# Turning a later token tile's normalised rows, latents and rotary keys by three DMA transposes in place of nineteen on TensorE

## The reference

```python
xn = layernorm(x)
q  = rmsnorm(xn @ w_qa) @ w_qb          # 384 latents, 16 heads of 128 + 64
kv = xn @ w_kva                         # 128 latents and 64 rotary numbers
k_rope = kv[..., 128:] * cos + rotate_half(kv[..., 128:]) * sin
kv = rmsnorm(kv[..., :128]) @ w_kvb
scores = (q_nope . k_nope + q_rope . k_rope) * scale, causal softmax, @ v, @ w_o
```

## Time and profile before

| | us |
|---|---|
| runs | 1167.91, 1171.23, 1172.15 |
| median | 1171.23 |
| profiled execution, span from first to last instruction | 1169.4 |
| main loop, first `scores` to last | 162 to 853 |

### The profile page before, as it was taken

One profiled execution on the slowest core, in us unless ns is written; L12 is line 12 of the kernel. 1 busy time (PEld: TensorE's weight loads), 2 busy tenths in 40 slices (PEclk: granted clock), 3 DMA queues, 4 the chain that ended last, 5 costly groups with the idle time before them and its releaser, 6 DMA issues.

```text
span 1169.4 us, 18715 instructions
## 1 busy us (share of the span) xinstructions
PE 980.4 (84%) x6106; PEld 574.0 (49%) x6124; DVE 959.2 (82%) x2669; ACT 678.1 (58%) x1449; POOL 296.4 (25%) x524
## 2 busy tenths in 40 slices
PE   0446667899999999999999999999978655559997
PEld 0234444555555555555555555555545544435553
DVE  5757749989989888989998988888868898866885
ACT  1446557667667666756666666656512676754442
POOL 1036533223223223222322222213100113221211
PEclk9769779999999999999999999999989888769999
DMA  9300003433323336334335244336363520001333
GB/s 350 139 1 1 1 8 73 75 59 71 71 59 67 66 62 142 62 64 69 65 68 138 55 68 60 64 67 140 68 218 86 168 91 19 0 1 36 84 80 91
DMA packets 217328, 90.78 MB, mean 78 GB/s; under 512 B 191496, under 2 KB 202760, under 8 KB 216720
## 3 DMA queue, kind: packets, MB, share of 16 engines
q1 hardware_dynamic: 217232, 89.58, 33.5%
HBM read 36.06 MB, written 7.34 MB: 37 GB/s over the span
## 4 chain that ended last, share of the span: by engine, by line
PE 53%; DVE 30%; ACT 6%; issue 5%; POOL 3%; DMA 3%; SPq 0%; DVEq 0%; ACTq 0%; POOLq 0%
PE bank L1930 13%; PE bank L1880 8%; PE bank L1915 6%; PE bank L1828 3%; PE bank L1859 3%; DVE arena L709 2%; PE bank L1898 2%; DVE arena L711 2%; PE bank L1901 2%; PE bank L1899 2%; PE bank L1900 2%; PE bank L1902 2%; DVE arena L791 2%; DVE arena L675 2%; DVE arena L1529 2%
## 5 line engine op out<-in xcount | busy, mean ns | idle before, releaser
L1218 ACT ACTIVATE arena<-bank,arena,scal 128x128 f32<-128x128 f32 (+3 forms) x256 | 157.7, 616 | 112.7 <-POOL arena L1059 111.6
L1930 PE MATMUL bank<-arena 128*128 128x512 f16 x768 | 179.1, 381 | 1.9 <-DVE arena L1562 1.9
L1536 DVE SCALAR_TENSOR_TENSOR arena<-arena 128x128 f16<-128x128 f32 (+3 forms) x256 | 142.2, 555 | 9.1
L1059 POOL TENSOR_TENSOR arena<-arena,scal 128x1 f32<-128x1 f32 x256 | 51.7, 203 | 347.4 <-DVE arena L1512 345.7
L1880 PE MATMUL bank<-arena 128*128 128x512 f16 x576 | 137.6, 385 | 0.0
L1529 DVE TENSOR_SCALAR arena<-arena 128x128 f16<-128x128 f32 (+3 forms) x256 | 125.4, 490 | 7.4 <-DVE arena L1521 0.8
L1512 DVE TENSOR_REDUCE arena<-bank 128x1 f32<-128x128 f32 (+3 forms) x256 | 123.7, 483 | 7.8 <-PE bank L1903 6.7
L1915 PE MATMUL bank<-arena 128*128 128x512 f16 (+3 forms) x768 | 117.7, 304 | 11.5 <-DMA arena<-arena 5.8
L1930 PEld LDWEIGHTS bank<-arena 128*128 128x128 f16 x768 | 72.9, 98 | 81.0 <-issue 4.4
L1915 PEld LDWEIGHTS bank<-arena 128*128 128x128 f16 x768 | 71.8, 99 | 63.0 <-issue 16.5
L1237 ACT ACTIVATE arena<-bank 32x512 f32<-32x512 f32 x128 | 75.3, 588 | 26.0 <-PE bank L1859 24.7
(11 more groups left out here) (201 smaller groups left out, 2049.5 us busy)
## 6 DMA issues: line engine op xcount, KB each, us to landing
arena<-in_L_attn_w_qb SPq DMA_DIRECT2D x1, 4608.0 KB, 21.6
arena<-arena SPq DMA_TRANSPOSE x272, 2.7
arena<-in_x SPq DMA_DIRECT2D x4, 1024.0 KB, 6.9
arena<-in_L_attn_w_o SPq DMA_DIRECT2D x1, 4096.0 KB, 31.9
arena<-in_fside_BxS2xS SPq DMA_DIRECT2D x4, 1024.0 KB, 8.8
arena<-in_L_ffn_w SPq DMA_DIRECT2D x8, 512.0 KB, 7.6
out<-arena SPq DMA_DIRECT2D x16, 256.0 KB, 2.3
arena<-in_x SPq DMA_DIRECT2D x12, 256.0 KB, 3.0
```

Source lines behind the costliest of these rows:

```text
L1218: act.activation(pf(k), banks[S_BANKS[G % 3]][:, 0:n], ACT.Exp, bias=NB[:, k:k + 1], scale=sc_exp, accum_out=SUM[:, k:k + 1]).then_inc(s_e ...
L1536: dve.scalar_tensor_tensor(out=ph_part(k, 1), in0=pf(k).rearrange("p (t c) -> p t c", c=P), scalar=R4[:, k:k + 1], in1=ph_part(k, 0), op0= ...
L1930: last = pe.matmul(banks[Y_BANK][:, :], ot(gp, a, k, (q & 3) * P, P), wo(b, gp * GH + k), start=(k == 0 and n == 0), stop=(k == GH - 1 and ...
```

## The change

For tiles 4 to 15 nothing is turned on PE any more. SP issues `turn_norm` (XH to XNT, 8 blocks), and `turn_latents` (KN, 3 blocks, and CH, 8 blocks, straight into the batch's store). `turn_norm` of the first of these tiles stands ahead of all other transposes; of the others it stands in the odd pair's step 7, between `turn_probs` of steps 6 and 7. `turn_latents` stands in the even pair's step 4, ahead of that step's `turn_probs`. With the transposes go `prep_te` on ACT, `prep_out` on DVE and their places in the order. Tiles 0 to 3 keep the old way.

```diff
@@ sync
+            def turn_norm(n):
+                sp.wait_ge(xn_lo, n + 1)
+                sp.wait_ge(kv_mm, n)
+                sp.dma_start_transpose(XNT.rearrange("p (a q) -> p a q", a=8), XH).then_inc(xn_in, 16)
+            def turn_latents(n):
+                par, tile = (n >> 2) & 1, n & 3
+                sp.wait_ge(kr_made, n + 1)
+                sp.dma_start_transpose(part_kr(par, tile), KN).then_inc(kr_in, 16)
+                sp.wait_ge(ch_lo, n + 1)
+                sp.dma_start_transpose(part_ct(par, tile), CH).then_inc(ct_in, 16)
             load_xt(TB)
             for i in range(NPAIR):
                 for g in range(8):
+                    if i == 0 and g == 0:
+                        turn_norm(TB)
+                    if g == 7 and i & 1 and i // 2 + 1 + TB < NT:
+                        turn_norm(i // 2 + 1 + TB)
+                    if g == 4 and i % 2 == 0 and i // 2 + TB < NT:
+                        turn_latents(i // 2 + TB)
                     turn_probs(i, g)
@@ scalar
             def prep_hi(n):
                 act.wait_ge(xn_made, n + 1)
-                if not (n == 0):
+                if n > TB:
+                    act.wait_ge(xn_in, 16 * (n - TB))
+                elif not (n == 0):
                     act.wait_ge(xn_t, n)
...
                     if (j, g) == (0, 0):
-                        if prep is not None:
-                            prep_te(prep[0])
                         qn_hi_(2 * i + 1, 1)
@@ vector
             def prep_rope(n, tile):
...
-                if not (n == 0):
+                if n > TB:
+                    dve.wait_ge(kr_in, 16 * (n - TB))
+                elif not (n == 0):
                     dve.wait_ge(kr_t, n)
...
             def prep_split(n):
                 dve.wait_ge(cf_made, n + 1)
+                if n > TB:
+                    dve.wait_ge(ct_in, 16 * (n - TB))
+                elif not (n == 0):
+                    dve.wait_ge(ct_t, n)
                 if not (n == 0):
-                    dve.wait_ge(ct_t, n)
                     dve.wait_ge(cn_made, n)
...
                     if (j, g) == (0, 6):
                         row_scale(G + 5, 5)
-                        if prep is not None:
-                            prep_out(*prep)
@@ tensor
             def prep_mm(n):
-                pe.wait_ge(xn_te, n + 1)
+                if n < TB:
+                    pe.wait_ge(xn_te, n + 1)
+                else:
+                    pe.wait_ge(xn_in, 16 * (n - TB) + 16)
+                    pe.wait_ge(cf_made, n)
...
-            def rope_mm(i, prep=None):
-                if prep is not None:
-                    pe.wait_ge(kr_te, prep[0] + 1)
+            def latents_in(b, front, turned):
+                if b == 0:
+                    pe.wait_ge(front, TB)
+                else:
+                    pe.wait_ge(turned, 16 * TB * b)
+            def rope_mm(i):
                 bp = (i >> 3) & 1
-                pe.wait_ge(ct_te, 4 * (i >> 3) + 4)
+                latents_in(i >> 3, ct_te, ct_in)
...
-                    pe.wait_ge(kr_te, 4 * (i >> 3) + 4)
+                    latents_in(i >> 3, kr_te, kr_in)
...
                     if (j, g) == (0, 0):
...
-                        if prep is not None:
-                            prep_t(prep[0])
...
-                    if (j, g) == (0, 6):
-                        if prep is not None:
-                            prep_t2(prep[0], i + 1)
```

More of the change, by code:

```diff
@@ L185, in decoder_layer @@
         tab_t, tab_made = sem("tab_t"), sem("tab_made")
+        xn_in, ct_in, kr_in = sem("xn_in"), sem("ct_in"), sem("kr_in")
         y_mm, y_added, xa_in, xa_out = sem("y_mm"), sem("y_added"), sem("xa_in"), sem("xa_out")
@@ L1971, in pair @@
                         if not last:
-                            rope_mm(i + 1, prep if j == 1 else None)
+                            rope_mm(i + 1)
                         if started(i - 5):
```

## The result

The changed kernel took **1174.64 us** (median of 10 runs, 1172.12 to 1175.65), the kernel before 1169.71 (10 runs, 1167.91 to 1172.15): ratio 1.0035, with a 95% interval of 1.0024 to 1.0046. It is slower by 4.9 us, where 2.9 us less had been forecast: inside the range of 1161 to 1177, but to the other side of the kernel before. The profiled execution took 1175.26 us, with a span of 1173.5 against 1169.4.

A forecast was written before the change was run, and what follows sets the result against it. PE was taken as the bound, with DVE close behind. Three early tiles at +1.01 us and nine later ones at -3.9 gave -2.9 us, from 1171.2 to 1168.3 us, range 1161 to 1177.

The forecast's parts named there:

- The bound: Steady tile of the main loop: PE sets the pace, its matmuls covering 44.48 of 44.66 us, DVE 40.10.
- the 1.25 us removed: PE, each tile: transposes of 0.45 and 0.62 us and a wait of 0.18 go, 15.0 us over 12 tiles.
- Chain 2: From `prep_mm`'s start over DVE to the first `values`, 13.02 us: 0.48 of the 0.80 us arrive.
- Chain 1: From `rope_mm`'s end over DVE to `prep_mm`'s start: the 0.45 us saved become an idle wait, PE gains -0.02.
- The early tiles' sum: Pairs 0, 2 and 4: a gain of 1.33 us, losses of 0.98 and 1.36, together +1.01 us.
- rival 3: Clock falls to half after idle ahead of `prep_mm` in pairs 2 and 4: 3.4 us more, 1171.7; chance 0.16.
- DVE is late: Pair 14, one of nine tiles counted at 0.46 us gain each: 0.2 us less gain there.
- The copies' 0.86 us on DVE: DVE's two removed copies: 0.86 us gained in each of pairs 0 and 2, where DVE sets the pace.
- The start of pair 2's `prep_mm`: Waiting for the DMA transpose, it may begin at 211.78 where it began at 209.94: 1.84 us late.
- Rival 1: PE keeps what it saves: the whole 15.0 us arrive, 1156.2 us; chance 0.25 for all beyond 5.9 us.
- Rival 2: `turn_norm`'s landing stands in PE's way 11 times; 0.9 us later each time would give 1178.2 us; chance 0.17.

The follow-up runs named there:

- experiment 3: The changed kernel with only latents and keys turned by DMA, the normalised rows back on PE: 1164.35 us, 0.9964 to the kernel before.
- experiment 1: The changed kernel with dummy matmuls filling PE's wait ahead of `prep_mm` in pairs 2, 4 and 14: 1170.37 us, 1.0004 to the kernel before.
- experiment 4: The changed kernel with only the normalised rows turned by DMA, latents and keys back on PE with DVE's copies: 1176.76 us, 1.0060 to the kernel before.
- experiments 2 and 7: 2: changed kernel, `turn_norm` issued ahead of step 6's `turn_probs`, 1163.44 us; 7: that plus experiment 6's swap and dummy matmuls in pairs 2 and 14, 1165.20 us.
- experiment 6: The swap: the changed kernel with DVE's `qn_lo_` moved ahead of `probs_hi` in the even pair's step 6: 1173.48 us, 1.0042 to the kernel before.

## Why the prediction was wrong, and where it was right

- **The bound and the chains: right.** PE is the bound; what it saves is caught by the two chains. In the steady tile PE waits ahead of `prep_mm` for the transpose and is idle 44.27 - 43.72 = 0.55 us in the period (0.8 forecast); of the 1.25 us removed 0.38 arrives.
- **Chain 2: right**, 13.01 us for 13.02, 0.48 us in experiment 3, and `values` 0.15 us behind `out_lo`, as it was worked out. Partly this was luck: two more things that the prediction didn't have come almost as late, the landing of the step-3 probabilities by 0.01 to 0.05 us and ACT's exponentials by some 0.2 us, and a longer one would have set the time.
- **Chain 1: right in mechanism, mis-sized by 0.1 us.** `prep_mm` begins 4.66 us after the issue of step 6's transpose (525.41), 4.56 forecast: the landing took 3.25 us, not the 3.1 of the earlier trace rows. Over nine tiles some 0.9 us.
- **The early tiles' sum, "+1.01 for three tiles": the step that failed.** The three came to -0.44 + 3.65 + 3.16 = +6.37 us, 5.4 more. Three terms were wrong. *The clock* was not in it at all: I had seen the 3.8 and 2.3 us of idle in pairs 2 and 4, had their price (rival 3, 1.7 us each; 1.6 measured), and left it out of the sum, as a rival with a chance of 0.16. The wait of 1.86 us with the half clock behind it spoke for it, as did that of 2.61 us with the stretch at 245.4; against it spoke those of 1.50 us and of 1.86 and 2.58 us in pair 1, behind which the clock stayed. So the rows left it open, and a sum that puts it at nothing needed a reason that they didn't give. I also missed the third place, pair 14, where the forecast only says "DVE is late": PE had waited 1.20 us there before, and with the 0.45 us that it had saved and DVE 0.35 later than before this became 1.99; how late DVE is there hangs on the reload of x, so this place was in part chance. Together 4.4 us by experiment 1, 2.8 of them in the three early tiles. *The copies' 0.86 us on DVE*, taken as a gain in pairs 0 and 2, gave nothing (experiment 3, and pair 0 after, whose 0.44 is no more than the 0.46 of experiment 4, which keeps the copies): DVE's next op then ran into POOL's. That this is why nothing came is read from the 0.74 us; the swap, which gave 0.47 of it back, could not show it in the time. That is 1.7 us. I had said of an edit costed at nothing what covers it, and had not asked what the copies covered. *The start of pair 2's `prep_mm`*: 2.40 us late where 1.84 was forecast, since SP's issue of step 6's transpose took 1.67 us there and the landing 0.1 to 0.2 more.

```profile
207.32 1.67 SPq L1013 DMA_TRANSPOSE arena<-arena  x1
```

- **The sum.** Forecast -2.9; the clock +4.4, the copies +1.7, chain 1 +0.9 and pair 2's start +0.6 make +4.7. The medians differ by +4.9 and the profiled spans by +4.1; pair 20 alone gave 0.7 us more than forecast.
- **Rival 1** (PE keeps all) was out by the rows cited against it. **Rival 2** (the landing decides): in this kernel no landing of `turn_norm` was over 3.3 us, so it did not come; experiments 2 and 7 show landings of 4.6 to 4.9, so its "for" was real. **Rival 3** is what happened, with three stretches for two, on top of early tiles that cost more than its sum had.
- **The Trainium skill's rule** ("VectorE: DVE Perf Modes", section "Rules for kernel authors": 128x128 on TensorE where PSUM will do) agrees with the trace for the normalised rows, whose consumer waits for them: +0.60% by DMA. It does not for latents and keys, which nobody needs for a tile's time: -0.36% by DMA, and there the measurement decides. In these kernels it is the slack of the consumer that tells, not the time of the transpose.

## What to carry to other kernels

Work that is taken off the bounding engine but leaves a dependence behind becomes an idle wait, and a wait of about 2 us can bring half clock for the 3.4 us that follow, or not: price both, the wait alone and the wait plus 1.6 us, and look at the places where the engine already waits 1 us or more. Put a DMA transpose where its result isn't wanted soon, and where it is, one place earlier in the queue can be worth more than the change itself (here 1174.6 to 1163.4 us). Before removing an op from VectorE, look at what GpSimd does at that moment and which op will stand there instead.

## What I had not expected of the hardware

- A cast of 128x64 took 1.26 us beside a GpSimd op and 0.19 without; a `tensor_scalar` of 128x256 took 1.23, 0.76 or 0.49 us by how much of the same GpSimd op was left; a subtraction that reads PSUM kept its 0.68 us beside it.
- The length of an idle wait does not tell whether half clock comes: 1.97 us brought it in experiment 1 (pair 22) and not in experiment 6 (pair 14); in the main loops of all thirteen traces the shortest wait that had a half-clock stretch at its end or behind it was 1.86 us and the longest that had none 2.59 us.
- `turn_norm`, 8 blocks, landed in 3.2 to 3.3 us in the changed kernel, and in up to 4.9 us in kernels where it stood one place earlier; the transpose of CH, 8 blocks too, took 3.2 to 4.8 us in the changed kernel itself. The issue of a transpose on SP took 1.2 to 1.3 us mostly, and 1.67 to 2.4 us at ten places of the loop.
